# A mixture of experts on routed tokens in place of all tokens, in a Flamingo-style gated stack

## What is computed

```
gates = softmax(xf @ gW + gb)                  # 8 experts
top2_scores, top2_idx = top_k(gates, 2)
w = (one_hot(top2_idx, 8) * top2_scores[..., None]).sum(1)
h = relu(einsum('nd,edf->enf', xf, W1) + b1)   # 128 -> 256
y = einsum('enf,efd->end', h, W2) + b2         # 256 -> 128
out = einsum('ne,end->nd', w, y)
```

## Time and profile before

| | |
|---|---|
| median of 3 runs | 723.52 us (722.88 to 726.53) |
| the profiled execution, span from first to last instruction (the page has no other time of it) | 724.5 us |
| busy: PE, weight loads, DVE, ACT, POOL | 93%, 69%, 71%, 56%, 37% |
| granted TensorE clock, mean | 0.983 |
| DMA | 12.72 MB, 18 GB/s |

### The profile page before, as it was taken

The page is one execution under the profiler, slowest core; times in us unless marked ns, Lnnn a source line. Parts: engine busy times, 40 slices in busy tenths (PEclk is TensorE's granted clock), DMA queues, the critical chain, the costliest instruction groups (busy, mean ns, idle before and its releaser), DMA issues.

```text
span 724.5 us, 19854 instructions
## 1 busy us (share of the span) xinstructions
PE 673.4 (93%) x8416; PEld 496.8 (69%) x8416; DVE 516.0 (71%) x1085; ACT 408.5 (56%) x680; POOL 265.6 (37%) x624
## 2 busy tenths in 40 slices
PE   6898889998999999999999999999999999998983
PEld 6777676676677776777777777677676667566552
DVE  0928745997968787988897868878889765674432
ACT  2353665456755675758666765475747474644331
POOL 6023531085226335452455334352524125113202
PEclk8989999999999999999999999999999999999997
DMA  5510000100000010000000000000000000000000
GB/s 152 155 53 2 2 2 2 30 3 23 24 3 1 2 44 24 3 2 1 24 2 15 3 2 25 1 2 2 10 17 1 2 10 8 1 16 1 1 15 15
DMA packets 24023, 12.72 MB, mean 18 GB/s; under 512 B 6432, under 2 KB 23424, under 8 KB 23936
## 3 DMA queue, kind: packets, MB, share of 16 engines
q1 hardware_dynamic: 21888, 10.52, 5.3%
q10 hardware_dynamic: 2048, 0.94, 0.5%
HBM read 9.36 MB, written 2.10 MB: 16 GB/s over the span
## 4 chain that ended last, share of the span: by engine, by line
PE 78%; DVE 9%; ACT 6%; POOL 3%; issue 2%; DMA 1%; ACTq 1%; POOLq 0%; SPq 0%; DVEq 0%
PE B L957 18%; PE A L957 17%; PE Y L957 17%; PE H L957 15%; PE B L1214 4%; PE A L961 2%; PE B L961 2%; ACT pool L468 1%; ACT A L468 1%; PE A L1110 1%; POOL hs L366 1%; ACT xn L473 1%; DVE stats L680 1%; DVE hax L660 1%; DMA y<-in_L_xattn_Wq_w_dram 1%
## 5 line engine op out<-in xcount | busy, mean ns | idle before, releaser
L957 PE MATMUL H<-xmT,w_s 128*128 128x512 f32 x256 | 135.4, 611 | 6.4 <-ACT pool L468 6.4
L957 PEld LDWEIGHTS Y<-w_s,pool 128*128 128x128 f32 x1024 | 121.4, 192 | 20.2 <-issue 15.8
L468 ACT ACTIVATE pool<-H,b_s 128x512 f32<-128x512 f32 x128 | 87.7, 685 | 82.8 <-PE H L957 82.1
L957 PE MATMUL Y<-w_s,pool 128*128 128x128 f32 x1024 | 126.6, 277 | 2.5 <-ACT pool L468 1.6
L934 DVE SCALAR_TENSOR_TENSOR pool<-Y,wgt,pool 128x128 f32<-128x128 f32 x256 | 71.8, 343 | 46.8 <-PE Y L957 46.6
L356 POOL TENSOR_TENSOR hs<-stats 128x4 f32<-128x4 f32 x48 | 13.3, 278 | 237.1 <-DVE stats L680 236.9
L957 PEld LDWEIGHTS H<-xmT,w_s 128*128 128x128 f32 x256 | 40.0, 190 | 26.3 <-ACT pool L468 15.3
L875 DVE TENSOR_REDUCE mx<-B 128x16 f32<-128x1024 f32 x32 | 39.0, 1220 | 24.9 <-PE B L957 24.8
L966 PE MATMUL H<-ident 128*128 128x128 f32 x379 | 51.1, 286 | 1.7 <-POOL ident L341 1.7
L957 PE MATMUL B<-hT,qT 32*64 32x256 f32 (+1 forms) x640 | 47.6, 374 | 4.3 <-ACT P L468 1.0
L366 POOL TENSOR_TENSOR hs<-hs,mhalf 128x4 f32<-128x4 f32 x48 | 49.8, 1037 | 3.8
(11 more groups left out here) (232 smaller groups left out, 1371.0 us busy)
## 6 DMA issues: line engine op xcount, KB each, us to landing
xin<-in_x_dram SPq DMA_DIRECT2D x8, 256.0 KB, 3.6
out_dram<-xb SPq DMA_DIRECT2D x8, 256.0 KB, 2.3
cin<-in_ctx_dram SPq DMA_DIRECT2D x7, 256.0 KB, 3.0
w_s<-in_L_ffn_W_dram SPq DMA_DIRECT2D x1, 1024.0 KB
min_<-in_mask_BxSxS_ik_dram SPq DMA_DIRECT2D x8, 128.0 KB, 2.4
cin<-in_ctx_dram ACTq DMA_DIRECT2D x1, 256.0 KB, 4.3
hh<-in_L_ffn_w_down_dram ACTq DMA_DIRECT2D x1, 176.0 KB, 5.5
hh<-in_L_ffn_w_gate_dram ACTq DMA_DIRECT2D x2, 64.0 KB, 5.4
```

The source lines that it names most:

```text
L468: return act.activation(dst, source, f, **kw)
L957: return pe.matmul(o, l, r, start=start, stop=stop)
```

## The change

The MoE is computed on routed tokens only. The groups form five parts (PARTS): three pairs, then group 6 and group 7 alone. For a part of n token tiles:
- `s_rank` gets five more VectorE instructions, which keep the first and the second choice apart.
- `i_cnt` (TensorE, n + 1 narrow matmuls: 9 or 5) counts for each token the tokens before it with the same expert; `i_pos` (VectorE, 17 instructions) makes of it each token's slot, experts rounded up to whole tiles of 128 slots, and the expert of each tile. The number of tiles is fixed: 23 for a pair, 15 for a single group, 99 in all.
- `i_sc` (GpSimd) writes each tile of tokens to its slots in DRAM by two indirect DMAs, 64 in all; `i_x` (SyncE) reads four tiles of slots back; `i_w` (SyncE) reads a tile's expert into a register and loads its W1, 128 KB, into one of 8 buffers.
- `m_x`, `m_h`, `m_y` (TensorE and ScalarE) transpose four tiles, make the hidden layer (2 matmuls of 128 columns for a tile, 2 activations of 128 columns) and the output (2 x 2 half sums, W2 chosen by a register that TensorE reads, one for a tile); SyncE's `m_y` stores four tiles.
- `e_g` (GpSimd) gathers the two rows of each token, 64 indirect DMAs in all; `e_cmb` (VectorE) adds them with their weights, 8 instructions for a group in place of 32.

The residual goes through DRAM (`r_st`, `r_ld`), both slot buffers are zeroed once in DRAM (`i_z`), some buffers are shared and waits added for that. All five lists of ORDER are written anew: the bulk of the DMA list l_1 stands behind the loads of x for groups 2 to 4, 55 fillers hold 378 transposes where 36 held 379, the first m_x stands among the stages of group 3's self attention, SyncE's list has 200 entries where it had 34 and GpSimd's 165 where it had 104. In GpSimd's list the 8 entries of `i_sc` of a pair stand nearly in a row, with two DMAs each, and the same holds for the four of an `e_g`. In VectorE's list `e_cmb:5` stands before `s_rank:7`.

```diff
+    CHUNKS = len(PARTS)
+    PART = {g: c for c, part in enumerate(PARTS) for g in part}
+    TG = [T * len(part) for part in PARTS]
+    TILES = [(2 * n * P + E * (P - 1)) // P for n in TG]
+    QUADS = [(n + 3) // 4 for n in TILES]
+    FIRST = [sum(TILES[:c]) for c in range(CHUNKS)]
+    FIRST_Q = [sum(QUADS[:c]) for c in range(CHUNKS)]
...
+    KEEP = 4
+    NW = 8
...
+    slots_x = [nc.dram_tensor("slots_x%d" % c, [TLM * P, D], F32) for c in range(2)]
+    slots_y = [nc.dram_tensor("slots_y%d" % c, [TILES[c] * P, D], F32) for c in range(CHUNKS)]
+    res_d = nc.dram_tensor("res_d", [NB * S, D], F32)
+    r_v = res_d[:].rearrange("(t p) d -> p t d", p=P)
...
-        w1_s = sb("w1_s", [E, FCH * P])
+        w1t = sb("w1t", [NW, FCH * P])
...
+        xm = sb("xm", [KEEP, T, P]); xmT = xT0; wgt = sb("wgt", [KEEP, T, E]); wT = sb("wT", [P])
         xb = sb("xb", [T, P])
-        pool = sb("pool", [2 * FCH * N + 2 * N])
-        hid = pool[:, 0:2 * FCH * N].rearrange("p (a c n) -> p a c n", a=2, c=FCH)
-        acc = pool[:, 2 * FCH * N:2 * FCH * N + 2 * N].rearrange("p (a t d) -> p a t d", a=2, t=T)
+        pool = sb("pool", [2 * 4 * FCH * P])
+        hid = pool[:].rearrange("p (a j c n) -> p a j c n", a=2, j=4, c=FCH)
...
+            if stage[0] == "m" and g == CHUNKS - 1 and k % 2:
+                return {"H": "A1", "Y": "B1"}[b]
...
-                    after(sp, v_mask, 2 * g)
+                    after(sp, v_c, 6 * (g - 1) + 1)
...
-                    sp.dma_start(w1_s[:], w1.rearrange("e d f -> d e f")).then_inc(ld_e, 16)
...
+                def r_st(g, k):
+                    sp.wait_ge(p_xb, g + 1)
+                    sp.dma_start(r_v[:, g * T:g * T + T, :], xs[:]).then_inc(s_res, 16)
+                def r_ld(g, k):
+                    sp.wait_ge(s_res, 16 * g + 16)
+                    after(sp, s_out, 16 * g)
+                    sp.dma_start(xb[:], r_v[:, g * T:g * T + T, :]).then_inc(ld_xb, 16)
+                def i_w(c, j):
+                    n = FIRST[c] + j
+                    if j == 0:
+                        sp.wait_ge(v_i, INDEXED * c + INDEXED)
+                    if n >= NW:
+                        pc = max(i for i in range(CHUNKS) if FIRST[i] <= n - NW)
+                        filled(sp, "m_h", pc, (n - NW - FIRST[pc]) // 2)
+                    e = sp.value_load(own[0:1, c % 2, j:j + 1], min_val=0, max_val=E - 1)
+                    sp.dma_start(w1t[:, n % NW, :], w1[bass.ds(e, 1)].rearrange("e d f -> d (e f)")).then_inc(ld_wt[n % NW], 16)
...
+                def i_z(c, k):
...
+                    for at_ in range(0, TLM, TB * 2):
+                        nt = min(TB * 2, TLM - at_)
+                        sp.dma_start(slots_x[c][at_ * P:(at_ + nt) * P, :].rearrange("(t p) d -> p t d", p=P), none[:, 0:nt, :])\
+                            .then_inc(s_zero, 16)
+                def i_x(c, q):
+                    n = FIRST_Q[c] + q
+                    nt = min(4, TILES[c] - 4 * q)
+                    sp.wait_ge(ld_sc[c], 32 * TG[c])
+                    if n >= 2:
+                        pq, pc = last_quad(n - 2)
+                        filled(sp, "m_x", pc, pq)
+                    sp.dma_start(xg[:, n % 2, 0:nt, :], slots_x[c % 2][4 * q * P:(4 * q + nt) * P, :].rearrange("(t p) d -> p t d", p=P))\
+                        .then_inc(ld_xg[n % 2], 16)
+                def m_y(c, q):
+                    n = FIRST_Q[c] + q
+                    nt = min(4, TILES[c] - 4 * q)
+                    freed(sp, "m_y", c, q)
+                    sp.dma_start(slots_y[c][4 * q * P:(4 * q + nt) * P, :].rearrange("(t p) d -> p t d", p=P), yq[:, n % 2, 0:nt, :])\
+                        .then_inc(s_yq[n % 2], 16)
...
-                    freed(pl, "e_bias", g - 1)
-                    filled(pl, "s_n5t", g - 1)
-                    pl.tensor_tensor(xm[:], y4[:], rep(rows[:, 8, :], 1, T), ALU.add).then_inc(p_xm, 1)
+                    after(pl, v_out, g - KEEP + 1)
+                    pl.tensor_tensor(xm[:, g % KEEP], y4[:], rep(rows[:, 8, :], 1, T), ALU.add).then_inc(p_xm, 1)
...
-                    freed(pl, "c_av", g)
-                    after(pl, s_out, 16 * g)
-                    pl.tensor_tensor(xb[:], xs[:, g % 2], rep(rows[:, 10, :], 1, T), ALU.add).then_inc(p_xb, 1)
+                    pl.wait_ge(x_n[4], g + 1)
+                    pl.tensor_tensor(xs[:], xs[:], rep(rows[:, 10, :], 1, T), ALU.add).then_inc(p_xb, 1)
...
+                def i_sc(c, t):
+                    if t == 0 and c == 0:
+                        pl.wait_ge(s_zero, 16 * LOADS_Z)
+                    if t == 0 and c >= 2:
+                        n = FIRST_Q[c - 1]
+                        pl.wait_ge(ld_xg[0], 16 * ((n + 1) // 2))
+                        pl.wait_ge(ld_xg[1], 16 * (n // 2))
+                    g = PARTS[c][t // T]
+                    pl.wait_ge(v_i, INDEXED * c + PLACED)
+                    pl.wait_ge(p_xm, 2 * g + 2)
+                    for k in range(2):
+                        pl.indirect_dma_start(out=slots_x[c % 2][:, :], out_offset=bass.IndirectOffsetOnAxis(ap=pos[:, c % 2, k, t:t + 1], axis=0),
+                                              in_=xm[:, g % KEEP, t % T, :], in_offset=None).then_inc(ld_sc[c], 16)
+                def e_g(g, t):
+                    c = PART[g]
+                    at_ = T * PARTS[c].index(g) + t
+                    if t == 0:
+                        n = FIRST_Q[c] + QUADS[c]
+                        pl.wait_ge(s_yq[0], 16 * ((n + 1) // 2))
+                        pl.wait_ge(s_yq[1], 16 * (n // 2))
+                        after(pl, v_cmb, 2 * g)
+                    for k in range(2):
+                        pl.indirect_dma_start(out=yg[:, k, t, :], out_offset=None, in_=slots_y[c][:, :],
+                                              in_offset=bass.IndirectOffsetOnAxis(ap=pos[:, c % 2, k, at_:at_ + 1], axis=0)).then_inc(ld_yg, 16)
...
-                def e_hid(g, k):
-                    e, c = divmod(k, FCH)
-                    filled(act, "e_hid", g, k)
-                    copy(hid[:, e % 2, c, :], H[:], ACT.Relu, bias=b1_s[:, e, c:c + 1]).then_inc(free["H"], 1)
...
+                def m_x(c, q):
+                    n = FIRST_Q[c] + q
+                    w_ = P * min(4, TILES[c] - 4 * q)
+                    filled(act, "m_x", c, q)
...
+                    if n >= 2:
+                        pq, pc = last_quad(n - 2)
+                        filled(act, "m_h", pc, min(2 * pq + 1, (TILES[pc] - 1) // 2))
+                    copy(xgT[:, n % 2, 0:w_], m_bank("m_x", c, q)[:, 0:w_]).then_inc(free[bank_of("m_x", c, q)], 1)
+                def m_h(c, p):
+                    q = p // 2
+                    n = FIRST_Q[c] + q
+                    filled(act, "m_h", c, p)
...
+                    if p == 0:
+                        act.wait_ge(v_i, INDEXED * c + INDEXED)
+                    if p % 2 == 0:
+                        after(act, s_yq[n % 2], 16 * (n // 2))
+                    for j in range(2 * p, min(2 * p + 2, TILES[c])):
+                        for h in range(FCH):
+                            at_ = 2 * P * (j % 2) + P * h
+                            last = copy(hid[:, n % 2, j % 4, h, :], m_bank("m_h", c, p)[:, at_:at_ + P], ACT.Relu,
+                                        bias=b1t[:, c % 2, h, j:j + 1])
+                    last.then_inc(free[bank_of("m_h", c, q)], 1)
+                def m_y(c, q):
+                    n = FIRST_Q[c] + q
+                    nt = min(4, TILES[c] - 4 * q)
+                    filled(act, "m_y", c, q)
+                    copy(flat(yq[:, n % 2, 0:nt, :]), m_bank("m_y", c, q)[:, 0:P * nt]).then_inc(free[bank_of("m_y", c, q)], 1)
...
+                    ve.tensor_scalar(picked[:, there, :], rank[:], 1.5, None, ALU.is_lt).then_inc(v_g, 1)
+                    ve.tensor_scalar(sel[:, 0, here, :], rank[:], 0.5, None, ALU.is_lt).then_inc(v_g, 1)
...
+                    ve.tensor_tensor(sel[:, 1, here, :], picked[:, there, :], sel[:, 0, here, :], ALU.subtract).then_inc(v_g, 1)
+                    ve.wait_ge(v_g, base + 14)
+                    ve.tensor_tensor(wsel[:], sel[:, :, here, :], rep(pe_[:], 1, 2), ALU.mult).then_inc(v_g, 1)
+                    ve.wait_ge(v_g, base + 15)
+                    ve.tensor_reduce(wk[:, PART[g] % 2, :, here], wsel[:], AX.X, ALU.add).then_inc(v_g, 1)
...
+                def i_pos(c, k):
+                    after(ve, v_i, INDEXED * c)
+                    base = INDEXED * c
+                    n, nt = TG[c], TILES[c]
+                    filled(ve, "i_cnt", c)
+                    ve.tensor_tensor(fills[:], rep(Y[:, n * E:n * E + E], 2, E), rep(steps[:], 1, E), ALU.is_gt).then_inc(v_i, 1)
+                    ve.wait_ge(v_i, base + 1)
+                    ve.tensor_reduce(ntile[:], fills[:], AX.X, ALU.add).then_inc(v_i, 1)
+                    ve.wait_ge(v_i, base + 2)
...
+                    ve.wait_ge(v_i, base + 7)
```

(79 more changed lines are left out.)

530 lines of the change are left out of this document (307 added, 223 removed).

## The result

The changed kernel takes 827.49 us, median of 4 runs (825.24 to 829.41), against 725.02 us for the kernel before on the same chip (722.88 to 726.87): ratio 1.141, 95% interval 1.137 to 1.144. The forecast was 678, and 632 to 735 as its range.

A forecast was written before the change was run, and what follows sets the result against it. The prediction took TensorE as full (396.14 of 400 us) with VectorE second, both nearly equally loaded after the change. A front of 585 us, register loads included, plus a tail of 93 gave 678 us, range 632 to 735.

The forecast's parts named there:

- The removal and the work: Busy sums to the last self attention: TensorE 626.1 - 184 + 78 = 520 us, VectorE 470, GpSimd 393.
- Up to the last self attention: Run's front: TensorE's and VectorE's shares add to 1.80, so 681 us take 378; with the first 200, 578 us.
- The forecast's own signs for the middle: Expected in the changed profile's middle: TensorE near 88% and VectorE near 80% busy.
- The clock: In the tail, TensorE may fall to 1.2 GHz during scatters: up to 15 us more, left to the range.
- The register loads: TensorE reading 99 experts: 0.43 us each, 30 us for 69 in the front, a quarter counted, 7 us.
- rival 2: Register loads stall TensorE in the open before each quad: 29 us more, 707 us; chance 0.13.
- rival 4: GpSimd becomes the bound, norms queued behind indirect DMAs; slower, 773 us at 2.59 us each; chance 0.10.
- D: Cost of each indirect DMA on GpSimd: 1.27 us in the forecast; slower by over 0.5% from 1.96 us.
- rival 3: SyncE's one list gates the tiles, weight loads, slot reads and stores waiting in order: 704 us; chance 0.07.
- TensorE alone still sets the pace: Both engines fill their room and register loads hide: 552 + 93 - 15 x 0.43 = 638 us; chance 0.20.
- The tail: From the last self attention to the end: 93 us where 66.7 stood, the trip through DRAM costing 26 more.

The follow-up runs named there:

- r1: Kernel before with the expert matmuls (e_hid, e_out) taken out and nothing put in; 695.8 us.
- f1: r1 with 640 transposes that nobody waits for in the places of the expert matmuls; 667.1 us.
- f2: r1 with 1280 transposes that nobody waits for in the places of the expert matmuls; 664.8 us.
- a_noload: Changed kernel without TensorE's 99 register loads, W2 block taken by tile number; 781.6 us.
- s_skeleton: Changed kernel without TensorE's register loads, with half of the indirect DMAs and few MoE matmuls; 774.7 us.
- p1_static: Changed kernel without TensorE's register loads, W1 kept in SBUF and no i_w; 777.0 us.
- x_w2_act: Changed kernel with each tile's W2 loaded by SyncE's DMA, no register on TensorE, and output slot stores issued by ScalarE; 814.2 us.
- p3_shell: Changed kernel without register loads, loads of W1 or indirect DMAs, and with few MoE matmuls; 749.6 us.
- r2: Changed kernel with the whole routed MoE taken out of its lists, shared buffers and residual through DRAM kept; 714.9 us.
- h2_double: Changed kernel with every matmul of the routed MoE's hidden layer and output made twice; 887.4 us.
- p2_noind: Changed kernel without any scatter or gather, a bias block combined instead; 812.2 us.
- b_halfind: Changed kernel with the second of each two indirect DMAs left out, 64 instead of 128; 814.3 us.
- v_double: Changed kernel with each of TensorE's 99 register loads made twice; 912.5 us, ratio to before 1.258.

## Why the prediction was wrong

**The removal and the work: right.** To the last self attention VectorE was forecast at 470 us and was busy 473.82. TensorE was forecast at 520, and 584.28 x 0.89, roughly its busy time in terms of full clock, is 520 (roughly, because 0.89 is the mean of a stretch with idle time in it). GpSimd: 1.27 us for an indirect DMA forecast, 0.98 + 0.30 to the next measured; 393 us in all forecast, 391 measured (356.87, and 0.30 behind each of 112 DMAs). The 1.27 was borrowed from an addition on the same engine, so that it fits this closely is luck. The sums of work were not what failed.

**The step that failed** is "Up to the last self attention": the two engines' shares would go on adding to 1.80, so that 681 us of work take 378. They added to 1.56 from 200 to 600 us ((333.69 + 291.28) / 400), and in r1, where nothing but removal was done, to 1.48. The 1.80 was there with the dense MoE, 184 us of TensorE's work up to that point, in the gaps of everything else. I took two full engines to be why the time was 658 us. With 184 us of TensorE's work out r1 still needs 651. With 63 us of transposes back in before this point (f1, 526 of its 640; clock 0.95) it is 623, with 126 us of them (f2, 0.98) 620. The forecast had 585, with the routed tiles in it. By its own rule f1, with 505 us of TensorE's work (626 - 184 + 63) and 436 of VectorE's, would be there at 552: 200 and (505 - 174.5 + 436 - 133.8) / 1.80. So the rule fails by 71 us where the clock is not in play. What sets the pace in its place is shown only in part: stages that wait for each other in lists written out by hand (the waits of r1 above). TensorE's work did count too, since before needs 38 us more than f2 up to here, with 184 us of experts in place of 126 of transposes, and VectorE's products. The forecast's own signs for the middle, TensorE near 88% and VectorE near 80% busy, read 83% and 73%.

The 123 us by which this front was missed (708 - 585) divide so, by the table above: 45 from the 578 that it gave without register loads to f1, which is this step; 49 from f1 to a_noload, at the same clock of 0.95, for the new lists and the routed work in them, which the forecast took to fit in for nothing beyond their busy time; and 29 for the register loads, 36 where it had counted 7.

**The clock** had only a sentence in the tail ("up to 15 us more"). It is worth 31 us in r1 (its time over that of f2), and it makes savings shrink: s_skeleton lost 72 us of matmuls and 81 us of GpSimd beyond a_noload and gained 7 us.

**The register loads** (rival 2) were priced at 0.43 us from the issue of a DMA, and all but those of the tail were counted at a quarter, 13 us in all. They are 0.64 each, 63 us in all, and leaving them out gives 46. So rival 2 had the mechanism and, with 43 us, nearly the size; its 707 stood on a front that was itself too short. That the size fits is partly luck: the price of a load was a third too low, and of the 63 us only 46 came back. The sign named for it, gaps of TensorE ahead of each m_x, shows at 11 of 26.

**GpSimd** (rival 4, the only one that ended slower) was wrong: D was 1.26 in the rows of the tail, not over 1.96, and the whole of the indirect DMAs is worth 15 us, 6 of them behind the last store. The one lengthened instruction that spoke for it stood beside a TENSOR_TENSOR of VectorE (326.19 to 327.40) and ended 0.09 us after it. **SyncE** (rival 3) was wrong as far as it was tried: 5 us for its registers and weight loads in p1_static, 2 for its stores in x_w2_act; its reads of slots were not taken out. The kernel came out slower by none of the rivals. A case in which much of the saved work was not in the way had no chance in the list, and "TensorE alone still sets the pace" had 0.20.

**The tail**: 93 us forecast, 119.8 measured. Its marks, answering to the earlier trace rows:

```profile
707.93 1.76 DVE L1091 RECIPROCAL rc<-B 128x256 f32<-128x256 f32 x1 [3.60 <-PE B L1229]
...
729.62 0.18 DVE L1146 SCALAR_TENSOR_TENSOR wgt<-rank,pe_ 128x32 f32<-128x32 f32 x1
...
738.47 1.11 POOL L554 DMA_INDIRECT slots_x<-xm,pos  x1 [3.59 <-DVE cmp L1183]
...
747.47 0.96 POOL L554 DMA_INDIRECT slots_x<-xm,pos  x1 [0.30 <-issue]
...
791.88 1.60 PE L1229 MATMUL B<-w_s,pool 128*128 x12 [0.84 <-ACT pool L597]
...
796.86 1.07 POOL L566 DMA_INDIRECT yg<-slots_y,pos  x1 [1.83 <-issue]
...
805.74 0.94 POOL L566 DMA_INDIRECT yg<-slots_y,pos  x1 [0.30 <-issue]
...
808.61 2.31 DVE L1205 SCALAR_TENSOR_TENSOR xm<-yg,wk,xm 128x128 f32<-128x128 f32 x8
```

| part of the tail | forecast | measured |
|---|---|---|
| to the gate weights (729.80) | 19.7 | 21.9 |
| ranks, counts, positions (738.47) | 4.7 | 8.7 |
| eight scatters (748.43) | 10.2 | 10.0 |
| landing, slots back, 15 tiles (793.48) | 29.5 | 45.0 |
| copy and store (796.86) | 2.3 | 3.4 |
| eight gathers (806.68) | 10.2 | 9.8 |
| landing and combination (810.92) | 5.9 | 4.2 |
| norm and residual, to the issue of the last store (818.96) | 8.0 | 8.0 |
| from there to the end of the span (827.70) | 2.7 | 8.7 |

The scatters and gathers were right to 0.4 us. The tiles were not, and their window says why:

```profile
748.43:761.33 12.90, 8.04 (x51) 7.32 (x51) 0.88 (x3) 5.40 (x16) 2.54 (x2) 0.87 0.50 143
761.33:793.48 32.15, 23.90 (x137) 21.60 (x138) 3.75 (x16) 14.51 (x43) 12.93 (x27) 0.73 0.43 124
```

Group 6's last 7 tiles are made behind the scatters instead of beside them, and group 7's 15 tiles take 32.15 us, 2.1 each where 1.44 were forecast (1.6 with ScalarE's 2 us at the end), at a clock of 0.73. The last row is 6 us that no instruction shows: see the last section.

**The account**, each figure the difference of two measured kernels. That it adds up is so by construction, since each kernel is taken from the next, and another order would divide it otherwise. From 827.5: TensorE's register loads 46 (a_noload), matmuls, W1 and indirect DMAs together 32 (p3_shell), the other routed work and its waits 35 (r2), the new lists, shared buffers and the residual through DRAM 19 (r1). Against that the dense MoE had cost 30 (before over r1). 46 + 32 + 35 + 19 - 30 = 102 us, the measured change (827.5 - 725.0 = 102.5).

## What to carry to other kernels

An engine at 99% in the middle of a kernel says that its queue is never empty, not that the time is its work. Before pricing a replacement for half of its work, run the kernel with that work taken out and nothing put in, and once more with work in its place that waits for nothing and that nobody waits for: here the two show that 224 us of matmuls, with VectorE's 72, were worth 30 us alone and 60 with the clock kept up. Any price of the new path is to be held against these. Work that can be done at any time keeps TensorE's clock up and fills others' waits; work that waits for an index, a register and two trips through DRAM did so far less here (h2_double).

## What the runs showed that was not expected

640 transposes that nobody reads made a kernel 29 us faster (695.8 to 667.1). They can help nothing but the clock, which went from 0.83 to 0.94. A register load on TensorE stands at 0.64 us in the open (2.55 us for four, 5.13 for eight), and 99 more of them cost 85 us of time, 0.86 each, more than their own length, with the clock down from 0.857 to 0.823.

From the issue of the last store to the end of the span there were 2.7 us in the kernel before, in r1, r2, p2_noind and p3_shell, none of which has an indirect DMA; 4.8 in b_halfind and s_skeleton, which have 64; and 8.7 in the changed kernel, a_noload, v_double and all other experiments that have 128. Nothing is shown in that time but the store. So 64 indirect DMAs cost 2 us and 128 cost 6 us once more, after the last instruction; what is done there stays open.
